# y^T of the first sequence by TensorE transposes, and a new order of the first and last steps, in a kernel of two cross-attentions

## The chip, the cores and the metric

The kernel runs on one NeuronCore of one Trainium2 chip. The metric is the device time of one execution in microseconds (us). The array clock of TensorE as granted is given in the profile as a share of 2.4 GHz.

## What is computed

There are 64 sequences, each with x (256 x 512) and a context c (256 x 256). Two cross-attentions follow each other; the second takes its softmax over the query positions and ends in a layer norm:

```python
# layer 0
Q = x @ Wq0 + bq0;  K = c @ Wk0 + bk0;  V = c @ Wv0 + bv0
y = x + softmax(Q @ K.T / sqrt(512), axis=-1) @ V @ Wo0 + bo0
# layer 1
q = y @ Wq1 + bq1;  k = c @ Wk1 + bk1;  v = c @ Wv1 + bv1
w = softmax(q @ k.T / sqrt(512), axis=queries)
z = y + w @ v
out = (z - mean(z)) * rsqrt(var(z) + 1e-6) * gamma + beta
```

## The kernel before, in words

The weights are folded once at the start: A0 = Wq0 Wk0^T, Bv = Wv0 Wo0, A1 = Wq1 Wk1^T and the vectors c0, c1 and g1 that come from the biases. Every operand of a product is kept as two halves, `_hi` (rounded, made by ScalarE) and `_lo` (the remainder, made by VectorE where the source is in PSUM and by GpSimd where it is in SBUF), and each product is three matmuls, hi*hi, hi*lo and lo*hi (`product`, L378).

One sequence n goes through these products on TensorE: `u_` (x^T by A0), `S0_` (the scores), `Pc_` (the exponentials by c; L411), `out_` in two halves q (by Bv; L422), `v_` (y^T by A1; L431), `S1_` (the scores of layer 1; L444), `wc_`, `s_` (the row sums of w; L454) and `pred_` in two halves. Four sequences are in flight. A body of the loop for sequence r issues `u_(r+3)`, `pred_(r-1)`, `Pc_(r+2)`, `S1_(r)`, `S0_(r+3)`, `out_(r+2)`, `v_(r+1)`, `wc_(r)`, `s_(r)`. There is no scheduler: every engine has a list of steps written out by hand, with semaphore waits inside the steps. What comes before the loop (the prologue) and the last four sequences, T(0) to T(3), have lists of their own.

Two operands have to be transposed between layers. The exponentials E0 and y are turned by VectorE in blocks of 32 x 32 (`E0_blocks`, `y_blocks`, L1032), written to DRAM by SyncE in four DMAs (`write_E0`, `write_y`, L265), and read back so that the blocks lie right (`read_E0`, `read_y`, L274). ScalarE then makes PT_hi and yT_hi (`PT_h`, `yT_h`, L731) and GpSimd PT_lo and yT_lo (`PT_l`, `yT_l`, L1473). Of the last sequence, y is transposed on TensorE instead (`yT_last`, L487; `yT_last_h`, `yT_last_l`): eight transposes of 128 x 128 into two PSUM banks.

A row of numbers g per sequence (y by g1) is computed by VectorE (`dot`, `g_blocks`), written to DRAM and broadcast to all partitions as gT (`write_g`, `read_g`, L281 to L292). It seeds the PSUM bank of `S1_` (`S1_seed_`, L745), so that `S1_` adds to it. `out_` and `pred_` have seeds as well.

y itself is formed in place in R by VectorE (`x1`, L1022, one call per half). After `pred_`, `x2` adds to R, `moments` and `spread` take mean and variance, GpSimd makes rstd and nmr (`scales`, L1485), ScalarE normalises (`normalise`, L818), and GpSimd multiplies by gamma and adds beta (`finish`, L1509; for T(2) `times_gamma` and `plus_beta`). The last sequence has a chain of its own at the end: `s_columns`, `add_s`, `x2_last`, `moments_last`, `spread_last`, `centre`, `finish_last` on VectorE (L1200 to L1187) with `scales_last` on GpSimd (L1494).

The PSUM banks that matter here: `s_bank` is bank 0, `Pc_bank` and `v_bank` are both bank 1, `S1_bank` is bank 5. `Pc_(n)` waits for v_lo(n-2), since v(n-2) has to be out of that bank, and `v_(n)` for Pc_lo(n+1).

## Time and profile before

| | us |
|---|---|
| runs of the kernel before | 1164.41, 1165.70, 1165.85 |
| median | 1165.7 |
| the profiled execution, its own time | 1164.51 |
| its span (first to last instruction) | 1162.6 |
| granted TensorE clock, mean over the span | 0.997 |

The profile's rows give the start and the duration of an instruction or of a run of equal ones (xN), its line, its operands as out<-in, and in brackets the idle time of the engine before it with what released it. Times are from the start of the span. Matmuls overlap in the rows, so that consecutive ones start closer than they last.

### The profile page before, as it was taken

Reading aid. Unit: us, or ns where it says so; the run is one execution under the profiler, and the core shown is the slowest. Engines: PE = TensorE matmul, PEld = TensorE weight load, DVE = VectorE, ACT = ScalarE, POOL = GpSimd, SP = SyncE. Lnnn points to the kernel's source line nnn. Section 1 sums busy time; section 2 is a strip of 40 time slices with the busy share of each in tenths; the row PEclk is TensorE's granted clock in tenths of the full one; section 3 lists DMA queues with packets and bytes.
Section 4 is the critical chain, followed back from the end, with each engine's and each line's share of the span. In section 5 each row is a group of like instructions: output and inputs, shape, how many; then the busy total and the mean of one; then the engine's idle time right before and its main releaser. Section 6 shows DMA issues by size and latency. Waiting matters only on the chain.

```text
span 1162.6 us, 25505 instructions
## 1 busy us (share of the span) xinstructions
PE 1137.9 (98%) x7917; PEld 1058.8 (91%) x7917; DVE 923.2 (79%) x2148; ACT 893.0 (77%) x1859; POOL 967.3 (83%) x768
## 2 busy tenths in 40 slices
PE   9989999999999999999999999999999999999995
PEld 7789999999999999999999999999999999999984
DVE  4667888878878878878878788887887887887887
ACT  3568788788788788778778878878878778877763
...
GB/s 314 202 186 204 218 230 210 217 240 209 213 233 214 214 238 210 213 235 213 219 227 227 211 217 230 211 216 231 219 211 237 211 212 238 210 214 236 191 120 68
DMA packets 131697, 249.05 MB, mean 214 GB/s; under 512 B 15696, under 2 KB 88912, under 8 KB 123344
## 3 DMA queue, kind: packets, MB, share of 16 engines
...
## 4 chain that ended last, share of the span: by engine, by line
PE 92%; DMA 2%; DVE 2%; POOL 2%; issue 1%; ACT 1%; SPq 0%; POOLq 0%; DVEq 0%; ACTq 0%
PE bank L382 88%; PE bank L522 1%; PE bank L460 1%; DMA yT_raw<-y_dram 1%; PE bank L548 1%; POOL Y L1515 0%; PE bank L529 0%; DMA y_dram<-y_blk 0%; SPq L270 0%; POOL Y L1518 0%; DMA PT_raw<-E_dram 0%; DVE y_blk L1037 0%; DMA gT<-g_dram 0%; POOLq L69 0%; DVE R L1029 0%
## 5 line engine op out<-in xcount | busy, mean ns | idle before, releaser
L1446 POOL TENSOR_TENSOR xT_lo<-IN,xT_hi 128x1024 fp32r<-128x1024 f32 (+1 forms) x64 | 153.5, 2399 | 25.3 <-ACT xT_hi L671 25.3
L1515 POOL TENSOR_TENSOR Y<-Y,gamma_b 128x512 f32<-128x512 f32 x124 | 157.8, 1294 | 19.6 <-ACT Y L824 19.6
L1518 POOL TENSOR_TENSOR Y<-Y,beta_b 128x512 f32<-128x512 f32 x124 | 157.8, 1295 | 0.0
L1446 POOL TENSOR_TENSOR yT_lo<-yT_raw,yT_hi 128x1024 fp32r<-128x1024 f32 x63 | 151.4, 2404 | 5.1 <-ACT yT_hi L671 5.0
L382 PE MATMUL bank<-yT_hi,A_hi 128*128 128x256 f32 x512 | 144.4, 282 | 2.4 <-issue 2.4
L382 PE MATMUL bank<-xT_hi,A_hi 128*128 128x256 f32 x512 | 144.8, 283 | 1.1 <-DVE A_lo L1218 1.1
L382 PE MATMUL bank<-xT_hi,A_lo 128*128 128x256 f32 x512 | 144.5, 282 | 0.0
L382 PE MATMUL bank<-xT_lo,A_hi 128*128 128x256 f32 x512 | 144.2, 282 | 0.0
L382 PE MATMUL bank<-yT_lo,A_hi 128*128 128x256 f32 x512 | 144.2, 282 | 0.0
L382 PE MATMUL bank<-yT_hi,A_lo 128*128 128x256 f32 x512 | 143.7, 281 | 0.0
L1446 POOL TENSOR_TENSOR cT_lo<-IN,cT_hi 128x512 fp32r<-128x512 f32 x64 | 82.5, 1289 | 62.2 <-ACT cT_hi L671 62.2
L671 ACT ACTIVATE bank<-c_b,Z 128x512 f32<-128x512 f32 x128 | 88.0, 689 | 49.1 <-DVE R L1116 45.5
L1116 DVE TENSOR_TENSOR R<-bank,R 128x512 f32<-128x512 f32 x126 | 86.5, 686 | 41.2 <-PE bank L382 41.2
L824 ACT ACTIVATE Y<-R,nmr,rstd 128x512 f32<-128x512 f32 x126 | 95.9, 809 | 23.0 <-POOL nmr L1492 23.0
L1446 POOL TENSOR_TENSOR C_lo<-IN,C_hi 128x512 fp32r<-128x512 f32 x64 | 83.7, 1309 | 33.6 <-ACT C_hi L671 33.6
L671 ACT ACTIVATE bank<-bv_b,scol 128x512 f32<-128x512 f32 x126 | 82.2, 683 | 34.6 <-DVE scol L1103 34.5
L382 PE MATMUL bank<-Bv_hi,PcT_hi 128*128 128x512 f32 x256 | 101.5, 397 | 1.9 <-DVE PcT_lo L988 1.9
L382 PE MATMUL bank<-V_hi,wcT_hi 128*128 128x512 f32 x256 | 101.3, 396 | 1.2 <-DVE wcT_lo L988 0.9
L382 PEld LDWEIGHTS bank<-yT_hi,A_hi 128*128 128x128 f32 x512 | 96.3, 188 | 5.6 <-issue 2.8
L382 PE MATMUL bank<-Bv_hi,PcT_lo 128*128 128x512 f32 x256 | 100.9, 394 | 0.0
L382 PE MATMUL bank<-V_hi,wcT_lo 128*128 128x512 f32 x256 | 100.7, 393 | 0.0
L382 PE MATMUL bank<-V_lo,wcT_hi 128*128 128x512 f32 x256 | 100.5, 393 | 0.0
...
## 6 DMA issues: line engine op xcount, KB each, us to landing
...
y_dram<-y_blk SPq DMA_DIRECT2D x252, 128.0 KB, 2.5
...
E_dram<-E_blk SPq DMA_DIRECT2D x256, 64.0 KB, 1.9
...
gT<-g_dram SPq DMA_DIRECT2D x64, 128.0 KB, 7.1
```

Of the source, the lines that this page charges most:

```text
L382: last = nc.tensor.matmul(dst, stat(a, t), mov(b, t), start=(not seeded and t == 0 and n == 0), stop=(t == k - 1 and n == 2), skip_group_c ...
L460: last = nc.tensor.matmul(s_bank[:, 0:S], ones[:, :], part[:, :], start=(t == 0), stop=(t == 1))
L522: last = nc.tensor.matmul(dst[:, k * L:(k + 1) * L], WqT[:, h, d * P:(d + 1) * P], WkT[:, h, :], start=(k == 0 and h == 0), stop=(h == HT ...
L548: last = nc.tensor.matmul(bank[6 + l][:, :], WvT0_s[:, h, l * P:(l + 1) * P], Wo0_s[:, h, :], start=(h == 0), stop=(h == HT - 1))
L671: return nc.scalar.activation(dst, src, ACT.Copy, **kw)
L824: nc.scalar.activation(Y[n.k % 2][:, q, :], R[n.k % 4][:, q, :], ACT.Identity, bias=nmr[:, q:q + 1], scale=rstd[:, q:q + 1]).then_inc(Y_se ...
L1116: nc.vector.tensor_tensor(R[n.k % 4][:, q, :], pred_bank[q][:, :], R[n.k % 4][:, q, :], ALU.add).then_inc(x2_set, 1)
L1446: return nc.gpsimd.tensor_tensor(dst, src, fp(hi), ALU.subtract)
L1515: nc.gpsimd.tensor_tensor(y[:, q, :], y[:, q, :], gamma_b[:, :], ALU.mult).then_inc(Y_mul, 1)
L1518: last = nc.gpsimd.tensor_tensor(y[:, q, :], y[:, q, :], beta_b[:, :], ALU.add)
```

## The change

The y of sequence 0 no longer goes to DRAM and back. After `Pc_(1)` TensorE transposes it into `s_bank` and `S1_bank` (`yT_first`), ScalarE and VectorE make its two halves (`yT_first_h`, `yT_first_l`), and `y_blocks`, `write_y`, `read_y`, `yT_h` and `yT_l` begin with sequence 1. `v_(0)` writes to `s_bank`, so `Pc_(2)` doesn't wait for it. Ahead of `v_(0)` stands one new matmul of `ones` by a row block of Bv, 512 columns, that overwrites `S1_bank`; the seed of `S1_(0)` waits for it. The lists of all five engines are in a new order in the prologue and in the last four sequences. The loop is as it was. The diff, with context left out:

```diff
@@ -29,6 +29,9 @@
         self.k, self.base = k, base
+    def first(self, of=0):
+        return self.base is None and self.k == of
@@ -188,9 +191,16 @@
         ident_zero, ident_set = sem("ident_zero"), sem("ident_set")
+        yT_first_full, yT_first_hi, flags_set = sem("yT_first_full"), sem("yT_first_hi"), sem("flags_set")
         yT_last_full, yT_last_hi = sem("yT_last_full"), sem("yT_last_hi")
...
         s_added, centred, Y_last = sem("s_added"), sem("centred"), sem("Y_last")
+        def v_in(n):
+            return s_bank if n.first() else v_bank
+        yT_first_bank = (s_bank, S1_bank)
@@ -265,7 +275,7 @@
         return
-    sp.wait_ge(y_blk_set, n.count())
+    sp.wait_ge(y_blk_set, n.count(back=1))
     for i in range(NB):
@@ -274,7 +284,7 @@
         return
-    sp.wait_ge(y_blk_out, n.count(64, 63))
+    sp.wait_ge(y_blk_out, n.count(64, 63, back=1))
     sp.dma_start(flat4(yT_raw), y_dram.rearrange("a d i x -> (a d) (i x)")).then_inc(yT_in, 16)
@@ -311,25 +321,23 @@
 load_IN(Seq(1))
-weights(WkT1_s, WkT1, wk1_in)
 weights(WqT1_s, WqT1, wq1_in)
 load_x(Seq(0))
+weights(WkT1_s, WkT1, wk1_in)
 load_IN(Seq(2))
 write_E0(Seq(0))
-load_x(Seq(1))
+weights(Wv1_s, Wv1, wv1_in)
 read_E0(Seq(0))
-weights(Wv1_s, Wv1, wv1_in)
 load_IN(Seq(3))
 write_E0(Seq(1))
+load_x(Seq(1))
+read_E0(Seq(1))
 load_IN(Seq(4))
-read_E0(Seq(1))
-write_y(Seq(0))
-read_y(Seq(0))
 write_E0(Seq(2))
+write_g(Seq(0))
 read_E0(Seq(2))
-write_g(Seq(0))
+read_g(Seq(0))
 write_y(Seq(1))
-read_g(Seq(0))
 read_y(Seq(1))
@@ -351,14 +359,14 @@
-store(T(-2))
 load_x(T(2))
 write_g(T(1))
+store(T(-2))
 read_g(T(1))
+load_x(T(3))
 write_E0(T(3))
-load_x(T(3))
+write_y(T(2))
 read_E0(T(3))
-write_y(T(2))
 store(T(-1))
@@ -413,7 +421,10 @@
     pe.wait_ge(C_lo, n.count())
-    first(pe, v_lo, n.count(back=2))
+    if n.first(2):
+        pe.wait_ge(Pc_lo, n.count(back=1))
+    else:
+        first(pe, v_lo, n.count(back=2))
     for l in range(LT):
@@ -432,12 +443,12 @@
     pe.wait_ge(yT_lo, n.count())
-    if n.plus(1).there():
+    if n.plus(1).there() and not n.first():
         pe.wait_ge(Pc_lo, n.plus(1).count())
-    else:
+    elif not n.first():
         pe.wait_ge(v_lo, n.count(back=1))
     for l in range(LT):
-        last = product(cols(v_bank, l), lambda a, t: A1[a][:, t, l * P:(l + 1) * P],
+        last = product(cols(v_in(n), l), lambda a, t: A1[a][:, t, l * P:(l + 1) * P],
                        lambda b, t: by_q(yT[b], t), DT)
@@ -575,8 +586,24 @@
+def yT_first(q):
+    if q == 0:
+        pe.wait_ge(ident_set, 1)
+        pe.wait_ge(c1_set, 1)
+    else:
+        pe.wait_ge(A1_lo, 1)
+    pe.wait_ge(x1_set, Seq(0).count(2, q))
+    for d in range(DT):
+        last = nc.tensor.transpose(yT_first_bank[q][:, d * P:(d + 1) * P], R[0][:, q, d * P:(d + 1) * P],
+                                   ident[:, :])
+    last.then_inc(yT_first_full, 1)
 def v_first():
     pe.wait_ge(A1_lo, 2)
+    pe.wait_ge(yT_lo, 1)
+    nc.tensor.matmul(S1_bank[:, :], ones[:, :], Bv[0][:, 0, :], start=True, stop=True).then_inc(flags_set, 1)
     v_(Seq(0))
@@ -597,10 +624,12 @@
 out_first()
+S0_(Seq(2))
 g1_product()
-S0_(Seq(2))
 u_(Seq(3))
 Pc_(Seq(1))
+yT_first(0)
+yT_first(1)
 out_(Seq(1), 0)
@@ -641,20 +670,20 @@
 S1_(T(1))
-Pc_(T(3))
 pred_(T(0), 0)
 pred_(T(0), 1)
+Pc_(T(3))
 wc_(T(1))
...
 out_(T(3), 1)
-s_(T(1))
 v_(T(2))
...
 yT_last(1)
+s_(T(1))
+S1_(T(2))
 pred_(T(1), 0)
-S1_(T(2))
+pred_(T(1), 1)
 v_(T(3))
-pred_(T(1), 1)
 wc_(T(2))
@@ -731,7 +760,7 @@
         return
-    act.wait_ge(yT_in, n.count(16, 15))
+    act.wait_ge(yT_in, n.count(16, 15, back=1))
     first(act, v_full, n.count(back=1))
@@ -740,7 +769,7 @@
     first(act, S1_full, n.count(back=1))
-    copy(flat(vT[0]), v_bank[:, :]).then_inc(v_hi, 1)
+    copy(flat(vT[0]), v_in(n)[:, :]).then_inc(v_hi, 1)
@@ -862,46 +891,52 @@
+def yT_first_h():
+    for q in range(ST):
+        act.wait_ge(yT_first_full, q + 1)
+        copy(yT[0][:, q * DT:(q + 1) * DT, :].rearrange("p a b -> p (a b)"), yT_first_bank[q][:, :]
+             ).then_inc(yT_first_hi, 1)
 def S1_seed_first():
-    act.wait_ge(A1_lo, 1)
+    act.wait_ge(flags_set, 1)
     act.wait_ge(rows_in, 16 * 4)
...
 xT_h_first()
-cT_h(Seq(0))
 A0_h(0)
 A0_h(1)
+cT_h(Seq(0))
 u_h_first()
...
 xT_h(Seq(1))
+cT_h(Seq(1))
 Bv_h(0)
+exps0(Seq(0))
 C_h(Seq(1))
 Bv_h(1)
-exps0(Seq(0))
-cT_h(Seq(1))
 u_h(Seq(1))
+xT_h(Seq(2))
+cT_h(Seq(2))
+PT_h(Seq(0))
 out_seed_first()
-cT_h(Seq(2))
-xT_h(Seq(2))
-PT_h(Seq(0))
+exps0(Seq(1))
 A1_h(0)
-exps0(Seq(1))
+Pc_h(Seq(0))
 V1_h()
-Pc_h(Seq(0))
-C_h(Seq(2))
 A1_h(1)
...
 xT_h(Seq(3))
+C_h(Seq(2))
 out_seed_(Seq(1))
 PT_h(Seq(1))
-cT_h(Seq(3))
 u_h(Seq(3))
-C_h(Seq(3))
 Pc_h(Seq(1))
 exps0(Seq(2))
-yT_h(Seq(0))
+cT_h(Seq(3))
+yT_first_h()
+C_h(Seq(3))
+PT_h(Seq(2))
 out_seed_(Seq(2))
-PT_h(Seq(2))
 v_h(Seq(0))
@@ -942,43 +977,43 @@
 out_seed_(T(2))
+Pc_h(T(2))
 yT_h(T(1))
-Pc_h(T(2))
+normalise(T(-1))
 exps0(T(3))
-normalise(T(-1))
 exps1(T(0))
+w_1_(T(0))
 w_h(T(0))
-w_1_(T(0))
+w_sums_h(T(0))
 v_h(T(1))
-w_sums_h(T(0))
 S1_seed_(T(1))
 wc_h(T(0))
+pred_seed_(T(0))
 PT_h(T(3))
-pred_seed_(T(0))
 exps1(T(1))
-Pc_h(T(3))
 w_1_(T(1))
...
 yT_h(T(2))
-w_sums_h(T(1))
+Pc_h(T(3))
 out_seed_(T(3))
 S1_seed_(T(2))
+w_sums_h(T(1))
 wc_h(T(1))
 normalise(T(0))
-pred_seed_(T(1))
 v_h(T(2))
 yT_last_h()
+pred_seed_(T(1))
 exps1(T(2))
...
 w_h(T(2))
+w_sums_h(T(2))
+S1_seed_(T(3))
 v_h(T(3))
-S1_seed_(T(3))
-w_sums_h(T(2))
 wc_h(T(2))
+normalise(T(1))
 pred_seed_(T(2))
...
 w_h(T(3))
-normalise(T(1))
 wc_h(T(3))
@@ -1057,7 +1092,7 @@
     dve.wait_ge(v_hi, n.count())
-    minus(flat(vT[1]), v_bank[:, :], flat(vT[0])).then_inc(v_lo, 1)
+    minus(flat(vT[1]), v_in(n)[:, :], flat(vT[0])).then_inc(v_lo, 1)
@@ -1277,10 +1312,17 @@
+def yT_first_l():
+    for q in range(ST):
+        dve.wait_ge(yT_first_hi, q + 1)
+        last = minus(yT[1][:, q * DT:(q + 1) * DT, :].rearrange("p a b -> p (a b)"), yT_first_bank[q][:, :],
+                     yT[0][:, q * DT:(q + 1) * DT, :].rearrange("p a b -> p (a b)"))
+    last.then_inc(yT_lo, 1)
 def y_blocks_first():
...
     dve.wait_ge(g1_full, 1)
-    y_blocks(Seq(0))
+    y_blocks(Seq(1))
@@ -1301,12 +1343,12 @@
 c1_parts()
+max0(Seq(0))
 Bv_l(0)
-max0(Seq(0))
+E0_blocks(Seq(0))
 Bv_l(1)
-E0_blocks(Seq(0))
+c1_()
 u_l(Seq(1))
-c1_()
 g1_parts()
@@ -1317,17 +1359,17 @@
 x1(Seq(0), 1)
-y_blocks_first()
 max0(Seq(2))
-u_l(Seq(3))
+g1_()
+dots_first()
 Pc_l(Seq(1))
 E0_blocks(Seq(2))
-g1_()
-dots_first()
+u_l(Seq(3))
+g_blocks(Seq(0))
 x1(Seq(1), 0)
-g_blocks(Seq(0))
 x1(Seq(1), 1)
-y_blocks(Seq(1))
+yT_first_l()
+y_blocks_first()
 v_l(Seq(0))
@@ -1367,58 +1409,58 @@
 dot(T(1), 1)
+g_blocks(T(1))
 u_l(T(3))
 x2(T(-1), 0)
-g_blocks(T(1))
 x2(T(-1), 1)
...
 spread(T(-1))
+Pc_l(T(2))
 max0(T(3))
-Pc_l(T(2))
 max1(T(0))
+x1(T(2), 0)
 E0_blocks(T(3))
-x1(T(2), 0)
 rz1_(T(0))
...
 y_blocks(T(2))
+w_sum_(T(0))
 w_l(T(0))
-w_sum_(T(0))
 dot(T(2), 0)
...
 s_columns(T(0))
+wc_l(T(0))
 g_blocks(T(2))
 max1(T(1))
-wc_l(T(0))
+x2(T(0), 0)
 rz1_(T(1))
+x2(T(0), 1)
+w_l(T(1))
+w_sum_(T(1))
+moments(T(0))
 Pc_l(T(3))
-x2(T(0), 0)
-w_sum_(T(1))
-w_l(T(1))
-x2(T(0), 1)
-moments(T(0))
 spread(T(0))
...
 x1(T(3), 1)
-s_columns(T(1))
 dot(T(3), 0)
...
 v_l(T(2))
+s_columns(T(1))
 yT_last_l()
+max1(T(2))
 x2(T(1), 0)
-max1(T(2))
 rz1_(T(2))
+x2(T(1), 1)
+w_sum_(T(2))
 w_l(T(2))
-w_sum_(T(2))
-x2(T(1), 1)
 moments(T(1))
+spread(T(1))
 v_l(T(3))
...
 max1(T(3))
-spread(T(1))
 rz1_(T(3))
@@ -1473,7 +1515,7 @@
         return
-    pool.wait_ge(yT_hi, n.count())
+    pool.wait_ge(yT_hi, n.count(back=1))
     minus(blocks(yT[1]), raw(yT_raw), blocks(yT[0])).then_inc(yT_lo, 1)
@@ -1530,21 +1572,20 @@
 cT_l(Seq(0))
+identity()
+C_l(Seq(0))
 xT_l(Seq(1))
-C_l(Seq(0))
-C_l(Seq(1))
 cT_l(Seq(1))
 xT_l(Seq(2))
+C_l(Seq(1))
 PT_l(Seq(0))
 cT_l(Seq(2))
+xT_l(Seq(3))
 C_l(Seq(2))
-xT_l(Seq(3))
 PT_l(Seq(1))
+cT_l(Seq(3))
 C_l(Seq(3))
-cT_l(Seq(3))
-yT_l(Seq(0))
 PT_l(Seq(2))
-identity()
 pool.wait_ge(rows_in, 16 * 4)
@@ -1575,8 +1616,8 @@
 PT_l(T(3))
+yT_l(T(2))
 w_sums_l(T(1))
-yT_l(T(2))
 scales(T(0))
```

## Rows read from the trace of the kernel before

**Rows 1.** The page, busy time, share of the span and instructions, first line.

```profile
PE 1137.9 (98%) x7917; PEld 1058.8 (91%) x7917; DVE 923.2 (79%) x2148; ACT 893.0 (77%) x1859; POOL 967.3 (83%) x768
```

**Rows 2.** Stretches: us, busy PE, PEld, DVE, ACT, POOL, granted clock, DMA share, GB/s.

```profile
57.20:59.60 2.40, 0.00 (x0) 0.01 (x1) 1.24 (x3) 1.38 (x2) 2.32 (x1) 1.00 0.35 74
...
67.00:1100.00 1033.00, 1032.94 (x7304) 970.00 (x7305) 836.56 (x1972) 830.69 (x1736) 905.03 (x713) 1.00 0.68 219
...
1155.00:1157.00 2.00, 0.00 (x0) 0.00 (x0) 2.00 (x2) 0.00 (x0) 2.00 (x2) 0.50 0.02 4
```

**Rows 3.** Timeline of TensorE, 54 to 73 us: start, us, instruction, idle before and releaser.

```profile
54.13 0.50 PE L382 MATMUL bank<-Bv_hi,PcT_hi 128*128 128x512 f32 x1 [1.41 <-DVE PcT_lo L988]
...
59.62 0.36 PE L382 MATMUL bank<-yT_hi,A_hi 128*128 128x256 f32 x1 [2.43 <-issue]
...
64.21 0.36 PE L382 MATMUL bank<-PT_hi,C_hi 128*128 128x256 f32 x1 [1.50 <-DVE vT_lo L988]
...
67.06 0.35 PE L382 MATMUL bank<-vT_hi,cT_hi 128*128 128x256 f32 x1 [1.18 <-ACT bank L671]
...
72.86 0.39 PE L382 MATMUL bank<-yT_hi,A_hi 128*128 128x256 f32 x1
```

**Rows 4.** The chain of waits, 45 to 78 us: start, us, what.

```profile
52.42 3.59 DMA yT_raw<-y_dram
...
56.04 1.07 ACT yT_hi L671
...
62.71 3.50 DMA gT<-g_dram
```

**Rows 5.** Timeline of SyncE's queue, 58 to 65 us.

```profile
58.67 0.68 SPq L285 DMA_DIRECT2D g_dram<-g_blk  x1
60.90 1.77 SPq L270 DMA_DIRECT2D y_dram<-y_blk  x4
...
64.49 0.34 SPq L278 DMA_DIRECT2D yT_raw<-y_dram  x1
```

**Rows 6.** Timeline of VectorE, 1139 to 1160 us.

```profile
1154.30 2.71 DVE L1179 SCALAR_TENSOR_TENSOR bank<-R,nmu,gamma_b 128x512 f32<-128x512 f32 x2
1158.73 1.41 DVE L1186 SCALAR_TENSOR_TENSOR Y<-bank,rstd,beta_b 128x512 f32<-128x512 f32 x2 [1.72 <-POOL rstd L1497]
```

**Rows 7.** Timelines of TensorE and of VectorE around 1130 us, the transposes of T(3).

```profile
1128.83 1.04 PE L495 MATMUL bank<-ident,R 128*128 128x128 f32 x8
...
1130.27 1.28 DVE L988 TENSOR_TENSOR yT_lo<-bank,yT_hi 128x512 fp32r<-128x512 f32 x2
```

**Rows 8.** Timeline of VectorE, 53 to 66 us.

```profile
57.73 0.71 DVE L1029 SCALAR_TENSOR_TENSOR R<-bank,rz,R 128x512 f32<-128x512 f32 x1
59.62 1.25 DVE L1037 STREAM_TRANSPOSE y_blk<-R 128x1024 f32<-128x1024 f32 x1 [1.19 <-POOL yT_lo L1446]
```

**Rows 9.** Timeline of GpSimd, 54 to 73 us.

```profile
61.54 1.27 POOL L1446 TENSOR_TENSOR PT_lo<-PT_raw,PT_hi 128x512 fp32r<-128x512 f32 x1 [2.02 <-ACT PT_hi L671]
...
70.41 2.39 POOL L1446 TENSOR_TENSOR yT_lo<-yT_raw,yT_hi 128x1024 fp32r<-128x1024 f32 x1
```

**Rows 10.** Timeline of GpSimd, 1138 to 1160 us.

```profile
1144.97 2.54 POOL L1515 TENSOR_TENSOR Y<-Y,gamma_b 128x512 f32<-128x512 f32 x2 [1.42 <-ACT Y L824]
...
1149.94 1.16 POOL L1490 TENSOR_TENSOR rstd<-ve,half 128x2 f32<-128x2 f32 x1
...
1154.75 3.37 POOL L1505 TENSOR_TENSOR Y<-Y,beta_b 128x512 f32<-128x512 f32 x2
```

**Rows 11.** Timeline of ScalarE, 1137 to 1153 us.

```profile
1140.78 1.30 ACT L671 ACTIVATE bank<-bv_b,scol 128x512 f32<-128x512 f32 x2 [1.59 <-DVE scol L1103]
...
1144.08 1.52 ACT L824 ACTIVATE Y<-R,nmr,rstd 128x512 f32<-128x512 f32 x2
```

**Rows 12.** Timeline of TensorE at 1139 us.

```profile
1139.21 0.36 PE L460 MATMUL bank<-w_sums_hi,ones 128*128 128x256 f32 x1 [0.65 <-POOL w_sums_lo L1446]
```

**Rows 13.** The page, DMA issues: count, KB each, median us to landing.

```profile
gT<-g_dram SPq DMA_DIRECT2D x64, 128.0 KB, 7.1
```

## The prediction

> **What bounds the kernel now.** I read the busy shares first. TensorE is busy for 1137.9 of 1162.6 us [rows 1], so at most 24.7 us can be won without taking work away from it. The stretches come next [rows 2]: from 67 to 1100 us TensorE is busy for 1032.94 of 1033 us. Nothing in there can be shortened by this change, and whatever is won before 67 us is kept, because every other engine has slack in the loop. What is to be had lies in the start and after 1100 us. The third view is TensorE's own waits at the start [rows 3]: 1.41 us before `out_(1)`, 2.43 before `v_(0)`, 1.50 before `Pc_(2)`, 1.18 before `S1_(0)`, after which it never waits until the loop is over. `v_(1)` follows its predecessor at 72.86 with nothing between them. The chain of waits says why `v_(0)` is late: the y of sequence 0 goes out to DRAM and comes back (3.59 us for the read alone, 1.07 for the copy behind it), and the broadcast of g lands 3.50 us after its issue [rows 4]. That issue was not late by itself: SyncE had issued g's write at 58.67 and then stood behind the four writes of y(1) until 62.7 [rows 5]. At the other end the last thing is VectorE's `finish_last`, which had idled 1.72 us for GpSimd's rstd [rows 6].
>
> The profiled execution took 1164.5 us, 1.9 more than its span; the median of the runs shown is 1165.7, 1.2 above it. I sum against the profiled one and put the 1.2 back at the end.
>
> **The start, part by part.** Up to 52.6 us TensorE is continuously fed, and it stays so: of the reordered copies and loads I find none that would come later than its product (the nearest is PT(1), by some 0.9 us). The moved loads (WkT behind WqT and x(0), x(1) behind E0(1), IN(4) behind PT(1)'s read) are covered in the same way, by products; lost cover would cost the lateness one for one. The cost to that point is nothing.
>
> Transposes: eight were 1.04 us at the end of the kernel [rows 7]. They run from 52.7 to 53.7, in the 1.41 us in which TensorE waits anyway [rows 3]: nothing on the path. ScalarE's two copies come after `exps0(2)` and `cT_h(3)`, by my count done at 55.9, while `out_(1)` runs. VectorE's two subtractions took 1.28 us at the end [rows 7], but here they are queued behind `x1(1,1)`. That one waits for `out_(1,1)`, which ends at 57.19 (59.62 less the idle of 2.43 [rows 3]), and takes 0.71 us [rows 8]. So y^T(0) is there at 57.23 + 0.71 + 1.28 = 59.2. Before it was there at 59.6. The removed round trip therefore brings only 0.4 us, and the new 512-column product with `ones` ahead of `v_(0)` takes about 0.23 of it: `v_(0)` starts at 59.45, 0.15 earlier. Behind the waiting subtraction VectorE has `y_blocks(1)` and `v_l(0)`; the seed of `S1_(0)` now waits for the `ones` product too, which is done long before g is there.
>
> `Pc_(2)`: v(0) now goes to another bank, so the wait for v_lo(0) is gone. What is late next is PT_lo(2), at 62.81 [rows 9]; its chain is not touched (g's write goes ahead of the read of E0, in time that the read waits anyway). `Pc_(2)` starts at 62.85 instead of 64.21: 1.36 us.
>
> `S1_(0)`: it needs `Pc_(2)` done (62.85 + 1.45 = 64.3), v_lo(0) (64.2 as before [rows 3]) and the seed. The write of g now stands ahead of the read of E0(2) and its broadcast ahead of the four writes of y(1): g is ready at 56.1 and written when E0's writes are out, about 57.0; the broadcast is issued about 59.4, landed at 59.4 + 3.5 = 62.9 [rows 4], seeded behind `v_h(0)` at 63.9. `S1_(0)` starts at 64.3 instead of 67.06: 2.76 us.
>
> `v_(1)`: `S1_(0)`, `S0_(3)` and `out_(2)` take 72.86 - 67.06 = 5.80 us [rows 3], so it would be due at 70.1. But y^T(1) still takes the DRAM way. `y_blocks(1)` starts at 59.2 instead of 59.62 and takes 1.25 [rows 8]; the read follows the first write by 64.49 - 60.90 = 3.59 [rows 5], so it is issued at 64.05 and lands 3.5 later at 67.55; ScalarE's copy 1.07 and GpSimd's subtraction 2.39 [rows 4, 9], with the hops between them, make 71.1. `v_(1)` waits about 1.0 and starts at 71.1 instead of 72.86. **The start gives 1.75 us** (72.86 - 71.1), not 2.76; behind it I find nothing in iteration 0 or 1 that is due earlier than it is ready. Bounds: 0.15 if g lands as late as before or the read of y takes 2 us longer, 2.8 if the round trip is a microsecond quicker.
>
> **The end.** GpSimd's row is the one to look at [rows 10]: `finish(T1)` begins at 1144.97, `scales(T2)` is queued behind it until 1149.94, and the last `plus_beta(T2)` ends at 1158.12; only then come the two `scales_last`. It begins so late because ScalarE runs `normalise(T1)` at 1144.08, behind `pred_seed_(T2)`, `exps1(T3)` and `w_h(T3)` [rows 11]. The change puts it (and VectorE's `spread(T1)`) ahead of these. It then runs at about 1139.6, `finish(T1)` ends at 1145.6, `scales(T2)` follows its moments at 1148.0 and `plus_beta(T2)` ends about 1155.0. GpSimd is no longer last.
>
> Who is late next is VectorE: `add_s`, `x2_last`, moments, `centre`, `finish_last`. In there lie 1.72 us of idle and 1.3 us by which the two `centre` are longer (2.71) than two `finish_last` of the same size (1.41), while GpSimd adds beta beside them [rows 6, 10]. Both go: 3.0. Against it, `normalise(T1)` (1.52 us [rows 11]) now stands before `pred_seed_(T2)`, on the chain. That seed used to wait until 1140.74 for the columns of s(T2) [rows 11], whose sums were late by 0.65 [rows 12]; by the new order they are there about 0.6 earlier, at 1140.15. But `normalise(T1)` runs from 1139.6 to 1141.15, so the seed starts at 1141.15 instead of 1140.78: 0.4 later, and so down the chain through `exps1(T3)` to `pred_last`. `add_s` will again be stretched beside GpSimd, now by gamma instead of beta; I add 0.4. **The end gives 3.0 - 0.4 - 0.4 = 2.2 us.**
>
> The other exchanges between 1100 and 1139 (E0(T3)'s exponentials behind `normalise(T-1)`, its read behind the writes of y(T2), `pred_(T0)` ahead of `Pc_(T3)`, `moments(T0)` ahead of `Pc_l(T3)`) win and lose within 1.3 us each and end in a TensorE without gaps at `wc_(T2)`, within 0.3 us of before; they are in the 2.2. Bounds for the end: 0.5 (they cost a microsecond and `add_s` is stretched in full) to 3.2.
>
> Sum: 1.75 + 2.2 = 3.95. 1164.5 - 3.95 = 1160.6, and with the 1.2 of the median over the profiled execution, 1161.7; rounding toward the quicker bounds I say 1161.6.
>
> **Rivals.** (a) *The start gives nothing*: y(1)'s trip or g's broadcast takes its loop length instead of 3.5 us. For it: the median of all broadcasts of g is 7.1 us [rows 13]. Against it: no 1 MB load is issued just before it now. Only the 2.2 of the end and 0.15 remain: 1163.3.
> (b) *The end gives nothing*: VectorE's chain is pushed back by `normalise(T1)` as much as GpSimd's is relieved. For it: that step stands directly ahead of a chain step. Only the start remains: 1163.9, within what a measurement can tell from no change (0.2%, 2.3 us).
> (c) *The clock falls*, the rival on the slower side. The granted clock of this kernel stayed at the upper level, 2.4 GHz, through a stretch of 2.4 us without one product (57.2 to 59.6), and stood at 1.2 GHz only in the tail, at 1155 to 1157 [rows 2], long after TensorE's last product. In the changed kernel the gap before `out_(1)` holds only transposes, and 3 us of products later comes a gap of 2.2. If the clock fell at `v_(0)` and stayed low to `v_(1)`, the 10.1 us of products between (2.9 + 1.45 + 5.8) would take 20.2, and 1.0 of it would fall into the wait before `v_(1)`: 9.1 on top of the forecast, 1170.8. It decides from 5 us of products at the lower level (3.95 + 1.0). Against it is the trace: the same gaps, longer, with no fall.
> The Trainium skill, "TensorE: Matmul & The Clock Gate", Part 4, says that transposes don't count as busy for the gate, so that the filled gap would be as idle as the empty one; by that rule this change neither helps nor hurts, unless the two gaps are taken together. No row here can show it: at the end of the kernel the eight stand between dense products.
> (d) *More than forecast*: y(1)'s trip is quick and `v_(1)` hardly waits, and the end gives its upper bound: 2.8 + 3.2, 1159.7.
>
> **How the numbers follow.** Forecast 0.60, (d) 0.12, (a) 0.12, (b) 0.12, (c) 0.04. The forecast and (d) are faster by over 0.2%, (a) sits on that line and counts half, and of the forecast 0.02 falls short: faster 0.76; same 0.20; slower 0.04. To hold 8 in 10 the range reaches from (d) past (a) and (b), with a little for the spread of the runs shown: 1159.6 to 1164.4; (c) and the case that both ends of the bounds fall together are left out.
>
> **What would show it.** `v_(0)` preceded by an idle of about 2.0 us released by VectorE's yT_lo and not by GpSimd's; no idle before `Pc_(2)` beyond 0.5, released by PT_lo; `S1_(0)` at 64.3; a new wait of about 1 us before `v_(1)`, released by GpSimd's yT_lo; no wait of VectorE for rstd in the last 5 us, and `finish(T1)` over before 1147. I am wrong if `S1_(0)` is not before 66, if TensorE has new waits between 30 and 52 us, if a granted clock below 1.00 appears before 1150, or if GpSimd still ends the chain.

## The result, and the profile after

| | kernel before | changed kernel |
|---|---|---|
| median, us (5 runs each on one chip) | 1165.32 | 1159.76 (1159.66 to 1160.56) |
| ratio, 95% interval | | 0.9957 [0.9942, 0.9971] |
| the profiled execution, own time / span | 1164.51 / 1162.6 | 1160.45 / 1158.7 |
| mean granted clock of the profiled execution | 0.997 | 0.996 |

The change makes the kernel 0.43% faster. 1161.6 us was predicted, with 1159.6 to 1164.4 as the range; the median lies at its quick edge, where the prediction had put its rival (d). Between the two profiled executions the difference is 4.06 us, where the prediction's sum was 3.95. That these two agree so closely is in part luck: 0.98 us of the 4.06 lie ahead of `u_(0)` and are not the change's. The 1.8 us between forecast and median have another source; both are taken up below.

First TensorE's start in the changed kernel, to be held against [rows 3]. The timeline of TensorE, 51 to 71 us (start, us, instruction, idle before and releaser):

```profile
51.59 1.03 PE L599 MATMUL bank<-ident,R 128*128 128x128 f32 x8
53.17 0.50 PE L390 MATMUL bank<-Bv_hi,PcT_hi 128*128 128x512 f32 x1 [0.54 <-DVE PcT_lo L1023]
...
58.37 0.47 PE L606 MATMUL bank<-Bv_hi,ones 128*128 128x512 f32 x1 [2.13 <-DVE yT_lo L1023]
58.67 0.28 PE L390 MATMUL bank<-yT_hi,A_hi 128*128 128x256 f32 x1
...
63.03 0.28 PE L390 MATMUL bank<-PT_hi,C_hi 128*128 128x256 f32 x1
...
64.61 0.38 PE L390 MATMUL bank<-vT_hi,cT_hi 128*128 128x256 f32 x1
...
70.45 0.39 PE L390 MATMUL bank<-yT_hi,A_hi 128*128 128x256 f32 x1
```

The transposes lie in the gap before `out_(1)`, the wait before `v_(0)` is now for VectorE's yT_lo, and those before `Pc_(2)` and `S1_(0)` are gone. But `v_(0)` runs from 58.67 to 63.03, 4.36 us, where it took some 3.0 before. The stretches of the changed kernel show why (us, busy PE, PEld, DVE, ACT, POOL, granted clock, DMA share, GB/s):

```profile
67.00:1100.00 1033.00, 1032.97 (x7298) 969.20 (x7297) 836.89 (x1973) 830.13 (x1735) 905.09 (x714) 1.00 0.68 219
56.30:58.30 2.00, 0.00 (x0) 0.00 (x0) 1.92 (x3) 0.00 (x0) 0.37 (x1) 1.00 0.23 50
58.30:60.00 1.70, 1.64 (x11) 1.62 (x12) 1.25 (x1) 0.13 (x1) 0.00 (x0) 0.84 0.67 204
60.00:62.00 2.00, 2.00 (x11) 2.00 (x11) 0.00 (x0) 1.69 (x3) 1.28 (x1) 0.50 0.72 189
62.00:64.00 2.00, 2.00 (x16) 2.00 (x15) 0.14 (x1) 0.77 (x2) 0.00 (x0) 0.78 0.26 80
64.00:67.00 3.00, 3.00 (x26) 2.82 (x25) 2.96 (x8) 1.92 (x4) 1.56 (x1) 1.00 0.58 175
```

The granted clock fell to its lower level, 1.2 GHz, while `v_(0)` ran, and was back before `Pc_(2)` began. From 67 us on, TensorE is as full as before [rows 2].

The end, from the timelines of the changed kernel's ScalarE, GpSimd and VectorE, against [rows 6, 10, 11]:

```profile
1137.91 1.52 ACT L853 ACTIVATE Y<-R,nmr,rstd 128x512 f32<-128x512 f32 x2
1139.34 1.28 ACT L700 ACTIVATE bank<-bv_b,scol 128x512 f32<-128x512 f32 x2
```

```profile
1141.28 2.53 POOL L1560 TENSOR_TENSOR Y<-Y,beta_b 128x512 f32<-128x512 f32 x2
1145.97 0.70 POOL L1532 TENSOR_TENSOR rstd<-ve,half 128x2 f32<-128x2 f32 x1 [2.16 <-DVE nmu L1174]
...
1147.87 3.33 POOL L1543 TENSOR_TENSOR Y<-Y,gamma_b 128x512 f32<-128x512 f32 x2 [0.93 <-ACT Y L853]
1151.16 2.48 POOL L1547 TENSOR_TENSOR Y<-Y,beta_b 128x512 f32<-128x512 f32 x2
1153.60 1.67 POOL L1539 TENSOR_TENSOR rstd<-ve,half 128x1 f32<-128x1 f32 x2
```

```profile
1147.62 2.46 DVE L1238 SCALAR_TENSOR_TENSOR R<-bv_b,scol,R 128x512 f32<-128x512 f32 x2
...
1153.17 1.68 DVE L1214 SCALAR_TENSOR_TENSOR bank<-R,nmu,gamma_b 128x512 f32<-128x512 f32 x2
1154.77 1.40 DVE L1221 SCALAR_TENSOR_TENSOR Y<-bank,rstd,beta_b 128x512 f32<-128x512 f32 x2
```

`finish(T1)` is over at 1143.8 instead of 1150, GpSimd stands idle for VectorE (2.16) where it was queued, and the last `finish_last` follows `centre` with no wait. `centre` takes 1.68 instead of 2.71. The stretching neighbour has moved to `add_s`, now 2.46 (2.0 in the kernel before) beside gamma's 3.33.

**Where 4.06 us lie.** Two rows cut the run in three: the first product of `u_(0)` (the idle before it is 1.07 in both), and the first product of `s_` in the sixtieth loop iteration. Their rows in the changed kernel:

```profile
14.63 0.38 PE L390 MATMUL bank<-xT_hi,A_hi 128*128 128x256 f32 x1 [1.07 <-DVE A_lo L1253]
...
1093.34 0.28 PE L471 MATMUL bank<-w_sums_hi,ones 128*128 128x256 f32 x1
```

and in the kernel before:

```profile
15.61 0.39 PE L382 MATMUL bank<-xT_hi,A_hi 128*128 128x256 f32 x1 [1.07 <-DVE A_lo L1218]
...
1095.19 0.28 PE L460 MATMUL bank<-w_sums_hi,ones 128*128 128x256 f32 x1
```

To `u_(0)`: -0.98, because the clock rose to 2.4 GHz at 4.84 instead of 7.80 us and the warm-up products went quicker. That is no work of the new order: E7 and E8 below, which have it, rose at 7.8 and have `u_(0)` at 15.62, as before. From there to `s_`: 1078.71 against 1079.58, -0.87. From `s_` to the end of the span: 65.36 against 67.41, -2.05. Outside the span: -0.16. So 2.92 us in this pair lie where the change works. The next table gives these three numbers for every kernel, "start" being the distance from `u_(0)` to `s_`.

### The profile page after: what moved, and what is told of

The parts are those of the page before. It is cut to its first block, busy times and chain, and to the rows that moved or that the text cites. A ratio compares the mean times of both kernels' runs of the same rounds, so it can differ in the third digit from the quotient of the medians.

```text
span 1158.7 us, 25547 instructions
## 1 busy us (share of the span) xinstructions
PE 1139.7 (98%) x7926; PEld 1060.5 (92%) x7926; DVE 924.6 (80%) x2149; ACT 892.5 (77%) x1860; POOL 964.9 (83%) x767
## 4 chain that ended last, share of the span: by engine, by line
PE 94%; DVE 2%; DMA 1%; ACT 1%; issue 1%; SPq 0%; POOL 0%; DVEq 0%; ACTq 0%
PE bank L390 91%; PE bank L471 1%; PE bank L533 1%; PE bank L559 1%; DMA W_s<-in_W 1%; DMA yT_raw<-y_dram 0%; DVE w_lo L1117 0%; DVE R L1064 0%; DVE R L1238 0%; DVE stats L1159 0%; DMA y_dram<-y_blk 0%; ACT Y L853 0%; ACT bank L810 0%; DVE y_blk L1072 0%; DVE scol L1138 0%
## 5 line engine op out<-in xcount | busy, mean ns | idle before, releaser
L390 PE MATMUL bank<-Bv_lo,PcT_hi 128*128 128x512 f32 x256 | 100.5, 392 | 0.0
```

Of the source, the lines that this page charges most:

```text
L390: last = nc.tensor.matmul(dst, stat(a, t), mov(b, t), start=(not seeded and t == 0 and n == 0), stop=(t == k - 1 and n == 2), skip_group_c ...
```

## The experiments

Ratios are to the kernel before, timed beside each on the same chip. The stretches are those of one profiled execution each. "Fall" is where the granted clock fell in the profiled execution.

| kernel | median | ratio [95%] | `u_(0)` | start | tail | fall at |
|---|---|---|---|---|---|---|
| before | 1165.32 | | 15.61 | 1079.58 | 67.41 | none |
| changed | 1159.76 | 0.9957 [0.9942, 0.9971] | 14.63 | 1078.71 | 65.36 | 59.5 |
| E1 new start alone | 1162.83 | 0.9982 [0.9973, 0.9991] | 14.70 | 1077.89 | 67.31 | none |
| E2 new end alone | 1162.98 | 0.9975 [0.9966, 0.9984] | 15.91 | 1080.92 | 64.87 | 17.3, 61.7 |
| E3 fillers | 1160.76 | 0.9965 [0.9951, 0.9979] | 14.67 | 1079.17 | 64.86 | none |
| E4 y^T(0) sooner | 1160.01 | 0.9956 [0.9943, 0.9970] | 14.77 | 1079.10 | 64.93 | 63.3 |
| E5 transposes alone | 1165.59 | 0.9997 [0.9988, 1.0006] | 15.32 | 1080.78 | 67.90 | 15.4 |
| E6 g behind | 1160.81 | 0.9963 [0.9949, 0.9976] | 14.97 | 1079.10 | 64.93 | none |
| E7 normalise back | 1162.00 | 0.9969 [0.9957, 0.9981] | 15.62 | 1080.66 | 66.82 | 72.7 |
| E8 Pc_l first | 1159.47 | 0.9947 [0.9933, 0.9960] | 15.62 | 1080.53 | 64.15 | 72.7 |
| E9 order alone | 1165.50 | 1.0005 [0.9996, 1.0014] | 14.60 | 1082.55 | 65.15 | 59.5 (longer) |
| E10 y^T(1) by VectorE | 1159.72 | 0.9953 [0.9940, 0.9967] | 14.54 | 1079.39 | 64.87 | 59.8 |
| E11 seed first | 1161.48 | 0.9964 [0.9950, 0.9977] | 14.84 | 1079.91 | 65.95 | 59.8, 1145.3 |
| E12 three edits | 1158.94 | 0.9944 [0.9930, 0.9958] | 14.77 | 1077.86 | 64.16 | 60.0 |

**E1 and E2: the two halves.** E1 is the changed kernel with the lists of the last four sequences as before, E2 the kernel before with the new ones:

```diff
 # E1, each engine: the lists behind the loop
-            load_x(T(2))
-            write_g(T(1))
-            store(T(-2))
+            store(T(-2))
+            load_x(T(2))
+            write_g(T(1))
...
```

> The changed kernel with the last four sequences in the order of before: the start alone. My theory: start and end are separate and add up. The loop should begin as in the changed kernel (v_(1) at 70.45 less whatever the first clock rise shifts, the wait of iteration 1 for yT_lo(2) still there), and the end should take as long as before, so 0.9 us are won against before beyond the shift of the first clock rise: about 1164.4 where before is 1165.3. Rival: the medians (5.6 us apart) say more than the profiled pair, and the start brings 3 us of it: about 1162.3.

> The kernel before with the last four sequences in the new order: the end alone. My theory: from the last u_ product (1095.43 before) to the end of the span 65.1 us instead of 67.2, so 2.0 us are won: about 1163.3 where before is 1165.3. Rival: the end gives nearly all of what the medians show, 4 to 5 us: about 1160.8.

The product of the two ratios is 0.9957, that of the whole change: within their intervals the halves add up. For E1 the theory of 1164.4 missed, and the rival, that the medians say more than the profiled pair, was the nearer; E2 came within 0.4 of its theory. In E1's profile no clock falls, and the steps of the prediction can be read clean. TensorE in E1:

```profile
58.43 0.47 PE L606 MATMUL bank<-Bv_hi,ones 128*128 128x512 f32 x1 [2.13 <-DVE yT_lo L1023]
...
62.06 0.35 PE L390 MATMUL bank<-PT_hi,C_hi 128*128 128x256 f32 x1 [0.32 <-issue]
...
70.25 0.39 PE L390 MATMUL bank<-yT_hi,A_hi 128*128 128x256 f32 x1 [0.85 <-POOL yT_lo L1488]
```

Its start is 1.69 us shorter than before; 1.75 was predicted. E2's tail is 2.54 shorter; 2.2 was predicted.

**E3: does the fall of the clock cost anything?** Nine products of 512 columns, whose result nobody reads, fill the wait before `v_(0)`:

```diff
                 pe.wait_ge(A1_lo, 2)
+                pe.wait_ge(u_lo, 8)
+                for _ in range(9):
+                    nc.tensor.matmul(u_bank[:, :], ones[:, :], Bv[0][:, 0, :], start=True, stop=True)
                 pe.wait_ge(yT_lo, 1)
```

> The changed kernel with nine more 512-column products of ones by Bv into the u bank while TensorE waits for y^T(0), so that the gap of 2.13 us before v_(0) is filled. My theory: the granted clock does not fall at 59.5 us, v_(0) takes 2.9 us instead of 4.4, but v_(1) starts where it did (70.45), because yT_lo(1) comes by DRAM at 70.40: same time as the changed kernel within 0.3 us. Rival: the fall costs its 1.4 us to the end, and this kernel is 1.4 us faster than the changed one, about 1158.3.

The clock didn't fall in the profile, `v_(0)` took 3.0 us, and the median is not better than the changed kernel's (1.0 above it, with overlapping intervals; the theory allowed 0.3). `v_(1)` waited 1.46 us for y^T(1) instead. So up to `v_(1)` the wait for y^T(1) takes most of what the fall takes from `v_(0)`. E3's start is still 1079.17, 1.3 over E1's: 0.5 by y^T(1), which landed later, and 0.5 at iteration 6 and 0.2 later, for which I have no cause.

The price of the fall is better read from E1, which has the changed kernel's start and no fall. Its `v_(1)` is 0.27 us earlier, but its whole start is 0.82 shorter (1077.89 against 1078.71): 0.55 us more are lost behind `v_(1)`, between `Pc_(3)` and `wc_(2)`. VectorE and SyncE's queue in the changed kernel:

```profile
63.86 0.69 DVE L1023 TENSOR_TENSOR vT_lo<-bank,vT_hi 128x512 fp32r<-128x512 f32 x1 [4.26 <-ACT vT_hi L700]
...
66.65 0.44 SPq L257 DMA_DIRECT2D R<-in_x  x1
...
70.52 1.82 SPq L265 DMA_DIRECT2D E_dram<-E_blk  x4
75.95 0.34 SPq L273 DMA_DIRECT2D PT_raw<-E_dram  x1
```

and in E1:

```profile
62.41 0.69 DVE L1023 TENSOR_TENSOR vT_lo<-bank,vT_hi 128x512 fp32r<-128x512 f32 x1 [2.74 <-ACT vT_hi L700]
...
65.20 0.44 SPq L257 DMA_DIRECT2D R<-in_x  x1
...
70.33 1.80 SPq L265 DMA_DIRECT2D E_dram<-E_blk  x4
74.21 0.34 SPq L273 DMA_DIRECT2D PT_raw<-E_dram  x1
```

With `v_(0)` late, vT_lo is late, and g(1) behind it, and SyncE can send g(1), and the loads of x and IN that stand behind it, only 1.45 us later, while the write of E0(3) goes out nearly where it did. The read of E0(3) then follows its first write after 5.43 us instead of 3.88.

**E4: is `v_(0)` on the path?** VectorE makes y^T(0)'s low part ahead of `x1(1,0)`:

```diff
             g_blocks(Seq(0))
+            yT_first_l()
             x1(Seq(1), 0)
             x1(Seq(1), 1)
-            yT_first_l()
             y_blocks_first()
```

> The changed kernel with VectorE's two subtractions for y^T(0) ahead of x1(1,0) instead of behind x1(1,1). My theory: yT_lo(0) comes at about 56.2 instead of 58.2 and v_(0) follows out_(1) with no wait; y_blocks(1) starts at 57.6 instead of 58.35, so y(1) is back 0.75 us earlier and v_(1) starts at 69.7: 0.5 to 0.7 us faster than the changed kernel if y(2)'s trip follows, 0 if the wait of iteration 1 for y(2) takes it back. Before Pc_(2) there will be a wait for PT_lo(2) of about 2.5 us. Rival: the start is bound by g or PT(2), not by y(1)'s trip, and nothing changes at v_(1).

`v_(0)` began 42.0 us behind `u_(0)`, 2.0 earlier, and nothing came of it (0.9956 against 0.9957), where the theory had 0.5 to 0.7 us. `Pc_(2)` waited 2.29 us, and `v_(1)` began at 56.75 behind `u_(0)`, with a wait of 0.62 for y^T(1), whose read took longer here: 4.95 us from issue to ScalarE's copy, 3.39 in E1.

**E5 and E9: transposes and order, each alone.** E5 has the kernel before's lists and only the transposes; E9 has the new lists, but y^T(0) goes by DRAM:

```diff
 # E5, TensorE, in the old order
             Pc_(Seq(1))
+            yT_first(0)
+            yT_first(1)
 # E9, SyncE and GpSimd, in the new order
             load_IN(Seq(4))
+            write_y(Seq(0))
+            read_y(Seq(0))
             write_E0(Seq(2))
...
             cT_l(Seq(3))
+            yT_l(Seq(0))
             C_l(Seq(3))
```

> The kernel before, every engine's order and the whole tail as there, with only y^T of the first sequence by TensorE's eight transposes and the product that joins it to the row sums; its write and read through DRAM are left out. Theory 1 (what held the start was y(0)'s trip, and the reordering only makes it fit): v_(0) begins about as early as in the changed kernel, counted from the first product of u_(0), but g is still written behind the other transfers of SyncE's queue, so S1_(0) begins up to 1 us later than in the changed kernel; some 1.0 to 1.8 us of the start's 2.1 us are here, 1164.0 to 1164.8 beside 1165.8 for the kernel before. Rival (the order of the prologue is what gains, the transposes only pay for themselves): within 0.3 us of the kernel before.

> The changed kernel with its new prologue order and its new tail, but y^T of the first sequence by DRAM again: no transposes, no joining product; its write and read stand in SyncE's queue ahead of the write of E0(2), its two copies where the transposes' copies were. Theory (order and transposes are worth next to nothing alone and 1.7 us together, because each alone leaves the other's wait): y_blocks(0) waits for the product of g1, which stands later in this order, so v_(0) begins about 45.2 us behind the first product of u_(0) instead of 44.0, y_blocks(1) waits for y^T(0)'s low part, and v_(1) begins at 57.0 or later, as in the kernel before (57.25) instead of the 55.55 of the run with the new start alone; the time is that of the new tail alone, 1162.6 to 1163.4. Rival (the order is what gains, the transposes are not needed): v_(1) by 55.6 to 56.8 and 1160 to 1161.5.

Alone, the transposes bring nothing that can be measured (0.9997). In E5's profile `v_(1)` begins 58.43 us behind `u_(0)`; 1.52 of that is a fall of the clock inside `u_(0)` (4.64 us instead of 3.12), so 56.91 against 57.25 before. `S1_(0)` waited 2.16 us for the seed, since g still stood behind the queue.

Alone, the order costs: E9 has the new tail, worth 0.9975 in E2, and still comes out at 1.0005, so its start is 0.003, or 3.5 us, slower than the old one. Theory and rival both missed; the theory had 0. TensorE in E9:

```profile
62.60 0.55 PE L392 MATMUL bank<-yT_hi,A_hi 128*128 128x256 f32 x1 [6.41 <-POOL yT_lo L1486]
```

The writes of y(0) went out at 48.79, 0.8 us behind IN(4), which the old order issues 5.3 us ahead of them; the read could be issued only at 54.85, 6.06 us behind the first write, where it was 3.96 before. `v_(0)` begins 47.99 us behind `u_(0)`, and from there to `v_(1)` (60.12) TensorE waits for nothing more. So E9's start is set by the trip of y(0) itself, and by the fall of the clock, part of which lies in `v_(0)`; that E0(2) and g stood behind y(0) in the queue costs nothing in this trace.

**Each half of the start leaves a wait in place that the other removes; together they bring 1.7 us.** Against the old order, a `v_(0)` that starts sooner is not what the transposes bring (44.04 us behind `u_(0)`, against 44.01 before). In the new order they save 3.95 us at `v_(0)`, since the trip would be that much longer there. They also take a write and a read, and the wait between, out of SyncE's queue; E6 prices what g gains by its new place in it.

**E6: is g's place worth anything?**

```diff
             write_E0(Seq(2))
-            write_g(Seq(0))
             read_E0(Seq(2))
-            read_g(Seq(0))
+            write_g(Seq(0))
             write_y(Seq(1))
+            read_g(Seq(0))
             read_y(Seq(1))
```

> The changed kernel with SyncE's queue of g as before: g written behind the read of E0(2), read behind the write of y(1). Theory 1 (g's trip and y(1)'s trip are the two waits in series behind v_(0), and the second decides): g^T comes about 1 us later and S1_(0) with it, but v_(1) begins within 0.3 us of the changed kernel, because it waits for y(1)'s own trip (70.4 us in the changed kernel) which now starts up to 0.7 us earlier; the time is the changed kernel's within 0.5 us, 1160 to 1161. Rival (every us by which S1_(0) is late goes through to the end): 1.0 us or more slower, 1161 to 1162.

Without a fall of the clock, the start is 1.21 us longer than E1's: in the profile the rival is right. TensorE in E6:

```profile
65.91 0.36 PE L390 MATMUL bank<-vT_hi,cT_hi 128*128 128x256 f32 x1 [2.28 <-ACT bank L700]
...
71.72 0.39 PE L390 MATMUL bank<-yT_hi,A_hi 128*128 128x256 f32 x1
```

`S1_(0)` waits 2.28 us for its seed, which waits for g, and begins 50.95 us behind `u_(0)`, against 48.86 in E1. From there `v_(1)` follows with no wait, at 56.75 against 55.55. Of the 2.09 us by which `S1_(0)` is late, the wait of 0.85 that E1 has before `v_(1)` takes the first part, and the rest goes through. Behind the seed, ScalarE's copy xT_hi(4) is late too, and GpSimd, which keeps its own order, makes xT_lo ahead of yT_lo. Timeline of GpSimd in E6:

```profile
69.26 2.40 POOL L1488 TENSOR_TENSOR yT_lo<-yT_raw,yT_hi 128x1024 fp32r<-128x1024 f32 x1
```

yT_hi was ready at 68.31, and its low part began 0.95 late; it is done at 71.66, just as `v_(1)` is due, and delays nothing. The ratio alone, 0.9963, can't be told from the changed kernel's.

**E7: what the end hangs on.**

```diff
             wc_h(T(2))
-            normalise(T(1))
             pred_seed_(T(2))
             exps1(T(3))
             w_h(T(3))
+            normalise(T(1))
             wc_h(T(3))
```

> The changed kernel with one line of ScalarE's order moved back: normalise of sequence 1 of the last four behind w_h of the last one. Theory 1 (the end gains because GpSimd's finish of sequence 1 no longer pushes its last steps back): plus_beta of sequence 2 and the last rstd end some 2 us later, finish_last waits for rstd again by 1 to 2 us, and the time is 1.2 to 2.2 us over the changed kernel's, about 1161.7. Rival (the end gains by the order of VectorE and TensorE, and the place of normalise is of no account): within 0.4 us of the changed kernel, and finish_last without a wait.

The tail is 66.82: of the 2.54 us that the new end brings (E2), 1.95 hang on this one line. Its start has 1.5 us of a fall inside `v_(1)`, so that the median (1162.00) says less than the tail. VectorE in E7 has its old wait back, and its old slow `centre`:

```profile
1154.72 2.72 DVE L1214 SCALAR_TENSOR_TENSOR bank<-R,nmu,gamma_b 128x512 f32<-128x512 f32 x2
1159.15 1.41 DVE L1221 SCALAR_TENSOR_TENSOR Y<-bank,rstd,beta_b 128x512 f32<-128x512 f32 x2 [1.72 <-POOL rstd L1539]
```

E7 also shows what the new place of `normalise` costs. ScalarE's seed for `pred_(T2)` in E7:

```profile
1141.21 1.30 ACT L700 ACTIVATE bank<-bv_b,scol 128x512 f32<-128x512 f32 x2 [0.69 <-DVE scol L1138]
```

Counted from `s_(59)` that is 44.92 us, against 45.56 in E2, and `wc_(T3)` begins at 49.30 against 49.82: with `normalise` ahead, the seed is 0.64 us later and the chain behind it 0.5.

**E8: a wait that the new order made.**

```diff
+            Pc_l(T(3))
             moments(T(0))
-            Pc_l(T(3))
             spread(T(0))
```

> The changed kernel with VectorE's Pc_l of the last sequence ahead of moments of sequence 0 of the last four, which takes away the 0.49 us that out_ of the last sequence waits for it at 1120.93 in the changed kernel. Theory 1 (TensorE sets the end as far as its last product, so a wait of 0.49 us there is worth about that): 0.3 to 0.5 us faster. Rival (the 0.49 us comes back at the next wait, for VectorE's add_s and ScalarE's seed late in the tail, since those follow the softmax and not TensorE): within 0.15 us of the changed kernel, which the time hardly tells, with the waits behind 1140 longer by the same amount.

The tail is 64.15, 0.72 shorter than E2's. Theory 1 was right, and more than the wait of 0.49 came back. In the medians this is 0.3 us and not certain.

**E10: the next wait.** y^T(1)'s low part once by VectorE, which idles there, and not by GpSimd:

```diff
 # VectorE, first iteration
             max0(r.plus(3))
+            if not u:
+                yT_1_l()
             rz1_(r)
 # GpSimd
-            yT_l(r.plus(1))
+            if prefix:
+                yT_l(r.plus(1))
```

> The changed kernel with the low part of y^T of the second sequence, once, by VectorE (about 1.25 us) instead of GpSimd (2.40 us), in VectorE's idle time ahead of rz1 of the first sequence. Theory (what sets the start now is the second sequence's own trip through DRAM and its two copies, ended by GpSimd's): v_(1) begins 0.85 to 1.2 us earlier than with GpSimd, counted from the first product of u_(0), 54.7 to 55.7 instead of 55.55 to 56.8, and the time is 0.6 to 1.2 us under the changed kernel's. Rival (the next trip, that of y of the third sequence, or the products ahead of v_(1), takes the place): 0.2 us or less.

`v_(1)` no longer waits, and the median stays: the rival was right. But the clock fell in `v_(0)` here too, so that TensorE itself reaches `v_(1)` only at 55.56, where E1 has it; what the edit is worth without a fall no trace shows. TensorE in E10 waits one iteration later:

```profile
81.40 0.39 PE L390 MATMUL bank<-PT_hi,C_hi 128*128 128x256 f32 x1 [0.79 <-POOL PT_lo L1494]
```

and by `s_(59)` 1.57 us are lost (the loop from `s_(0)` to `s_(59)` takes 1019.52 us; 1017.95 in E1). SyncE's queue in E10 says what PT_lo(3) waited for:

```profile
66.36 0.44 SPq L257 DMA_DIRECT2D R<-in_x  x1
66.92 0.87 SPq L245 DMA_DIRECT2D IN<-in_packed  x1
...
70.22 2.45 SPq L265 DMA_DIRECT2D E_dram<-E_blk  x4
76.42 0.34 SPq L273 DMA_DIRECT2D PT_raw<-E_dram  x1
```

The read of E0(3) is issued 6.20 us after the first of its writes, which follow the loads of x and IN. In the changed kernel it is 5.43 us, in E1 3.88. What goes with it is how far ahead of the first write x was issued: 3.86 us in E10, 3.87 in the changed kernel, 5.13 in E1. Over all 13 kernels that load x there, one trace each: 3.6 to 4.0 us ahead, the read follows after 4.8 to 6.5; 4.8 to 5.2 ahead, after 3.1 to 4.8; 5.7 us and more ahead, after 3.1 to 3.4. The traces that lose time at `Pc_(3)` are the changed kernel's, E10's and E11's (0.5, 1.6 and 1.9 us by `s_(59)`), and in all three the clock fell in `v_(0)`.

**E11: is `normalise` in the way of the seed?**

```diff
 # on top of E8
             wc_h(T(2))
-            normalise(T(1))
             pred_seed_(T(2))
+            normalise(T(1))
             exps1(T(3))
```

> The run with Pc_l of the last sequence ahead, and in ScalarE's order pred_seed_ of sequence 2 of the last four ahead of normalise of sequence 1, where it was. TensorE's wait of 1.0 us for that seed at pred_ goes. Theory 1 (TensorE's waits in the tail are paid in full): the tail from s_ of the fifth sequence from the end to the end of the span, 64.15 us there, is 0.6 to 1.0 us shorter. Rival (the end hangs on the last sequence's softmax and on the four copies of the last S1, which start when they did; the prediction priced this step of the change at 0.4 us): within 0.2 us of it, up to 0.5 us longer if GpSimd, started 0.6 us later on finish, is last again.

Both theories missed: the tail is 1.80 longer than E8's. The seed waited 0.69 us for its columns and starts 0.63 us earlier than in E8, but now `normalise` stands between the seed and the last softmax. TensorE's wait moved one product on and grew:

```profile
1144.63 0.38 PE L390 MATMUL bank<-w_hi,C_hi 128*128 128x256 f32 x1 [1.82 <-DVE w_lo L1117]
```

Counted from `s_(59)`, this product begins 49.88 us on, against 49.08 in E8: 0.80 later. Behind it, in this execution, the clock fell (at 1145.26), and `wc_(T3)` took 2.2 us instead of 1.5. How much of the 2.0 us between the medians is the order and how much the clock is open.

**E12: what took the gain back.** E8's and E10's edits, and x(2) loaded while SyncE is idle (`x` is false in the first iteration):

```diff
             load_IN(Seq(4))
+            load_x(Seq(2))
             write_E0(Seq(2))
...
             write_g(r.plus(1))
-            load_x(r.plus(2))
+            if x:
+                load_x(r.plus(2))
```

> Three small edits together: Pc_l of the last sequence ahead of moments (as measured alone: the tail 0.75 us shorter), the low part of y^T of the second sequence by VectorE (as measured alone: v_(1) without a wait, but 1.6 us lost again by the third sequence's PT and y^T), and new: the load of x of the third sequence is issued in SyncE's idle time about 48.5 us, not at 65 to 66 us between the second sequence's y read and the fourth sequence's E0 write. Theory (what took the gain back is those transfers of x and IN in front of the write of E0(3), whose read was issued 6.2 us behind its first write there, 3.9 us in the run with the start alone): that distance is 4 us or less again, Pc_(3) waits for PT_lo by under 0.2 us, s_ of the loop leads the kernel before by 2.4 to 2.8 us, counted from the first product of u_(0) and without a clock fall, and the time is 1158.0 to 1158.9, against 1159.5 to 1159.8 for each edit alone. Rival (the DRAM trips of the second iteration are long by themselves, or IN's transfer is enough to hold them): the lead is 1.7 us or less and the time 1159.0 to 1159.6, from the tail alone.

SyncE's queue in E12:

```profile
66.71 0.36 SPq L245 DMA_DIRECT2D IN<-in_packed  x1
...
70.74 1.77 SPq L265 DMA_DIRECT2D E_dram<-E_blk  x4
73.84 0.34 SPq L273 DMA_DIRECT2D PT_raw<-E_dram  x1
```

3.10 us from write to read, no wait of TensorE before `Pc_(3)` or `v_(2)`, and a loop of 1017.95 us: nothing is lost behind the start. E10, whose clock fell at the same place, differs ahead of the tail by x(2) alone, and it lost 1.57 us there. So by one trace each it is x, issued shortly ahead of the trip, that took them. The start, 1077.86, is E1's (1077.89), though the clock fell in `v_(0)`. The lead over the kernel before is thus 1.72 us and not the 2.4 to 2.8 of the theory, which were for a start without a fall: `v_(1)` is at 55.60, as in E1. The median, 1158.94, is the best of the study, 0.8 under the changed kernel's; the intervals of the two ratios overlap, so that this kernel is better than the changed one is likely and not proven. It beats the kernel before by 0.56%.

## Why the prediction was right

Right, by its steps:

- *The start up to 52.6 us costs nothing*: from `u_(0)` to the transposes no wait is new (`u_(0)` to `v_(0)` is 44.0 us in both).
- *`Pc_(2)` 1.36, `S1_(0)` 2.76, `v_(1)` 1.75 us earlier, after a new wait of 1.0 for y^T(1)*: E1, counted from `u_(0)`, has 1.24, 2.59 and 1.70, and a wait of 0.85. Even where TensorE lost 1.4 us to the clock (the changed kernel's own profile), `v_(1)` was only 0.27 later than in E1, since the wait absorbed the rest.
- *`finish(T1)` over by 1145.6, `scales(T2)` at 1148.0, `plus_beta(T2)` over at about 1155.0*: with the 1.85 by which `s_(59)` is earlier added back, the rows say 1145.7, 1147.8 and 1155.5. *The end gives 2.2*: 2.05 in the profiled execution, 2.5 in E2, E3, E4, E6 and E10.
- *The terms of the end, 3.0 less 0.4 less 0.4*: from `centre` to the end VectorE takes 2.85 us less than before; from `add_s` to `centre` it takes 0.45 more. The third, `normalise(T1)` ahead of the seed, is there as well: by E7 the step costs the seed 0.64 and the chain 0.5. In the changed kernel's profile the seed is 0.41 later than before, counted from `s_(59)` (46.00 against 45.59); in E2 and its like it is where it was (45.56), since its columns come 0.7 earlier. That is where 2.05 and 2.5 part. With E8's edit the end gives 3.3.

Right with another content:

- *`v_(0)` 0.15 earlier*: it is not earlier at all, and E4 shows that it wouldn't matter. I had costed the transposes by what they do for `v_(0)` against the old order. E5 and E9 show that they and the new order are worth nothing or less apart, and E6 that 1.2 us of the start hang on g's place in SyncE's queue, for which y(0)'s trip makes room.

*The rivals*: (a) and (b) are out, since start and end each give their part (E1, E2). (d) names the right time for the wrong reason: `v_(1)` does wait, and the end gives 2.5 and not 3.2. (c) is below.

Wrong:

- *"Behind it I find nothing in iteration 0 or 1 that is due earlier than it is ready."* In E1 that holds. In the changed kernel's profile it doesn't: 0.56 us of the start's 1.43 (at `v_(1)`) are lost again by `s_(59)`, because y^T(2) and PT(3) are late. E0(3)'s write goes out 3.87 us behind the load of x, which the fall of the clock in `v_(0)` has moved towards it. E12 moves that load away, and the loss is gone although the clock falls. The prediction didn't count the loads as neighbours of the trip.
- *"I am wrong if a granted clock below 1.00 appears before 1150."* It did, and rival (c)'s mechanism is there; its price was not 9.1 us but 0.8 (the changed kernel's start against E1's, one trace each). Of the 1.4 us that `v_(0)` loses, 0.27 arrive at `v_(1)`, because the clock was back before `v_(0)` was over and the wait for y^T(1) lay behind; 0.55 come on top by the loads. In E7 and E8 it fell inside `v_(1)`, behind that wait, and there it was paid in full: `v_(1)` took 4.6 instead of 3.1. That it cost so little is in part luck: the 0.04 that the prediction gave it rested on one trace without a fall.
- *The 1.2 us of the median over the profiled execution, carried over unchanged*: this is the term that makes the 1.8 us. The changed kernel's median lies 0.7 below its profiled execution and not 1.2 above it. The profiled execution of before had no fall of the clock. Of the 61 executions of before that were timed beside the experiments, 9 had, like that one, a mean granted clock of 0.997, with a median of 1164.0 us; 41 had 0.995 or less, with medians of 1165.6 (0.995) to 1166.9 (0.993). With the new start and the old end (E1) 8 of 11 are at 0.997; with the transposes alone 1 of 11, with the order alone none of 11. So the new start takes away, in most executions, time at the lower clock that the old one's median holds. These counts show that much; which of the closed gaps does it they don't. The traces show falls at 15 to 17 us in two of the three kernels with the old order (E2, E5) and in none of the eleven with the new one.
